# A fused cross-attention and mixture-of-experts layer: the unused experts' bias added per tile on VectorE, and the context means formed through joined weights with sums on GpSimd

## The reference, cut to what matters

```python
x = x + tanh(g_xattn) * xattn(layernorm(x), ctx, ctx, mask, ...)      # B=8, S=256, D=128, 16 heads of 64
x = x + tanh(g_ffn)   * ffn(layernorm(x), W1, b1, W2, b2, Wr, br)     # 8 experts, hidden 512

# xattn: the context has 1601 rows; mask and a causal triangle leave 256 of them to look at
scores = where(mask, -1e30, q @ k.T / 8); scores = where(causal, -1e30, scores)
out = (softmax(scores) @ v) @ Wo + bo

# ffn: each token has one expert, but every expert adds its bias path for every token
indices = argmax(softmax(x @ Wr + br))
for i in range(8):
    m = (indices == i)
    h = relu((x * m) @ W1[i] + b1[i])
    out = out + (h @ W2[i] + b2[i])
```

## Time and profile before

| | before |
|---|---|
| device time, median of 3 runs | 433.3 us (424.26, 433.30, 433.83) |
| profiled execution | 424.33 us, its span 422.7 us |
| mean granted TensorE clock | 0.972 of full |
| busy: PE / DVE / ACT / POOL | 384.2 / 283.7 / 241.5 / 193.5 us |
| busy share: PE / DVE / ACT / POOL | 91% / 67% / 57% / 46% |
| DMA moved | 25.23 MB |

### The profile page before, as it was taken

One profiled execution on the slowest core, in us unless ns is written; L12 is line 12 of the kernel. 1 busy time (PEld: TensorE's weight loads), 2 busy tenths in 40 slices (PEclk: granted clock), 3 DMA queues, 4 the chain that ended last, 5 costly groups with the idle time before them and its releaser, 6 DMA issues.

```text
span 422.7 us, 11118 instructions
## 1 busy us (share of the span) xinstructions
PE 384.2 (91%) x2881; PEld 301.9 (71%) x2881; DVE 283.7 (67%) x1283; ACT 241.5 (57%) x888; POOL 193.5 (46%) x353
## 2 busy tenths in 40 slices
PE   3959658899999999999999999999999969899992
PEld 2836446777787787778777778877776758788882
DVE  3289999469839866983987597498847855344440
ACT  2665533547748774874778387477735424455441
POOL 7069962145345553543655355354525322534332
PEclk9998998999999999999999999999999995899998
DMA  7892469000000000000000000000000046322210
GB/s 198 213 334 78 135 207 305 0 3 2 1 26 0 0 12 12 0 0 25 0 0 10 15 0 0 25 0 0 0 26 2 2 149 265 100 58 64 75 36 6
DMA packets 20553, 25.23 MB, mean 60 GB/s; under 512 B 3545, under 2 KB 16677, under 8 KB 20528
## 3 DMA queue, kind: packets, MB, share of 16 engines
q1 hardware_dynamic: 18544, 19.40, 15.4%
q0 software_dynamic: 1984, 5.53, 3.5%
HBM read 18.48 MB, written 6.90 MB: 60 GB/s over the span
## 4 chain that ended last, share of the span: by engine, by line
PE 57%; DVE 23%; issue 11%; DMA 2%; ACT 2%; DVEq 1%; another core or an unknown queue 1%; POOL 1%; SPq 1%; ACTq 0%; POOLq 0%
PE ps_kv L1110 11%; PE ps_o L1110 10%; PE ps_w L1110 10%; PE ps_s L1110 8%; PE ps_t L1110 7%; PE ps_t L1183 6%; DVE masked L706 5%; PE ps_q L1110 4%; DVE prob_T L725 3%; DVE neg_max L706 2%; DVE rs_t L659 1%; DVE row_fix L713 1%; DMA wv_s<-in_L_xattn_Wv 1%; DVE rows L765 1%; DVE rs_t L657 1%
## 5 line engine op out<-in xcount | busy, mean ns | idle before, releaser
L543 ACT ACTIVATE prob<-masked,neg_max 128x128 f32<-128x128 f32 (+1 forms) x256 | 113.4, 444 | 80.5 <-DVE neg_max L706 80.4
L416 POOL TENSOR_TENSOR prob<-prob,row_inv 128x128 f32<-128x128 f32 x128 | 51.0, 398 | 150.2 <-DVE row_inv L719 150.2
L706 DVE CUSTOM_DVE_ANT_0 masked<-ps_s,mask_now 128x128 f32<-128x128 f32 (+1 forms) x256 | 78.3, 353 | 20.5 <-PE ps_s L1110 16.6
L418 POOL TENSOR_TENSOR prob<-prob,row_inv 128x256 f32<-128x256 f32 x128 | 78.3, 611 | 0.0
L725 DVE COPY prob_T<-ps_t 128x384 f32<-128x384 f32 x128 | 67.6, 547 | 0.0
L1110 PE MATMUL ps_s<-k_T,q_T 64*128 64x128 f32 (+1 forms) x512 | 60.7, 356 | 6.5 <-DVE neg_max L706 6.4
L1183 PE MATMUL ps_t<-ident,prob 128*128 128x128 f32 x384 | 58.1, 286 | 4.8 <-POOL prob L418 2.8
L1183 PEld LDWEIGHTS ps_t<-ident,prob 128*128 128x128 f32 x384 | 41.6, 143 | 27.5 <-issue 17.8
L1110 PE MATMUL ps_o<-prob_T,v_nat 128*64 128x256 f32 (+1 forms) x512 | 56.4, 342 | 0.0
L543 ACT ACTIVATION_READ_ACCUMULATOR prob<-masked,neg_max 128x1 f32 x256 | 47.8, 187 | 0.0
L1110 PEld LDWEIGHTS ps_s<-k_T,q_T 64*128 64x128 f32 x512 | 34.5, 190 | 17.1 <-issue 15.8
(11 more groups left out here) (194 smaller groups left out, 602.9 us busy)
## 6 DMA issues: line engine op xcount, KB each, us to landing
ctx_ring<-in_ctx SPq DMA_DIRECT2D x8, 768.0 KB
ctx_ring<-sorted_rows SPq DMA_DIRECT2D x24, 128.5 KB, 2.1
sorted_rows<-pad_rows POOLq DMA_DIRECT2D x6, 385.5 KB, 3.9
packs<-in_L_ffn_W SPq DMA_DIRECT2D x1, 2048.0 KB
packs<-in_L_ffn_W SPq DMA_DIRECT2D x8, 256.0 KB
ctx_nat<-in_ctx SPq DMA_DIRECT2D x8, 128.0 KB, 4.0
x_nat<-in_x SPq DMA_DIRECT2D x1, 896.0 KB, 9.3
sorted_rows<-pad_rows SPq DMA_DIRECT2D x2, 385.5 KB
```

The costliest lines, as they stand in the source:

```text
L416: g.tensor_tensor(prob[:, slot, 0:P], prob[:, slot, 0:P], row_inv[:, slot, 0:1].to_broadcast([P, P]), ALU.mult).then_inc(prob_ready, 1)
L418: g.tensor_tensor(prob[:, slot, P:W3], prob[:, slot, P:W3], row_inv[:, slot, 1:2].to_broadcast([P, S]), ALU.mult).then_inc(prob_ready, 1)
L543: s.activation(prob[:, slot, lo:hi], masked[:, slot % 2, lo:hi], ACT.Exp, bias=neg_max[:, slot, t:t + 1], scale=-1.0, accum_out=row_sum[:, ...
L706: v.tensor_tensor_reduce(out=masked[:, slot % 2, lo:hi], in0=ps_s[slot % 2][:, lo:hi], in1=mask_now[:, lo:hi], scale=-SCALE, scalar=FLOOR, ...
```

## The change

**First part.** The per-tile selector product is gone. `rest` is computed earlier: the 32 small products all run inside batch 7 (`EMPTY_AT`), the small product in step 6, and in step 7 eight products (`rest_everywhere`) spread `rest` over all 128 partitions, in two PSUM banks that ScalarE copies to `rest_all`. VectorE adds the chosen expert's row of `rest_all`, times tanh(g_ffn), to each loaded tile (`rest_to`), and `finish` waits for that.

**Second part.** The eight contexts share one buffer, loaded one at a time: context 0 where it was, the others in a loop on SP after the experts' weights, each after the sum of the one before. GpSimd does both additions for every context, one context per batch (step 3, for the next batch; context 0 after step 0 of batch 0), VectorE one reduction per batch (step 6). In batch 0 PE transposes Wv (8 transposes in steps 2 and 3) and multiplies it by Wo once (step 4), and transposes `blind` to columns. Then each batch has one product for its mean and one through the joined weights, with two copies on ScalarE, and GpSimd adds blind x mean to the residual rows: `residual_of` has three operations instead of one and moves from step 1 to step 4 (step 7 in batch 0). The two `blind` products of each output projection are gone. The tiles no longer share memory with the context ring.

```diff
-            for b in range(B):
-                r = b % CTXR
-                wait(sp, ctx_sum_ready, b - CTXR + 1)
-                sp.dma_start(ctx_ring[:, r, 0:FULL], ctx_in[b, 0:FULL * P, :].rearrange("(p j) d -> p j d", p=P)
-                             ).then_inc(ld_ring[r], 16)
-                sp.dma_start(tail_ring[0:TAIL, r], ctx_in[b, FULL * P:SK, :]).then_inc(ld_ring[r], 16)
+            sp.dma_start(ctx_buf[:, 0:FULL], ctx_in[0, 0:FULL * P, :].rearrange("(p j) d -> p j d", p=P)
+                         ).then_inc(ld_ctx, 16)
+            sp.dma_start(ctx_buf[0:TAIL, FULL], ctx_in[0, FULL * P:SK, :]).then_inc(ld_ctx, 16)
             sp.dma_start(w1_s, w1.rearrange("e d f -> d e f")).then_inc(ld_ffn, 16)
             for e in range(E):
                 sp.dma_start(w2_s[:, e], w2[e].rearrange("(c p) d -> p c d", p=P)).then_inc(ld_ffn, 16)
             sp.dma_start(b2_s[:, :], b2).then_inc(ld_ffn, 16)
+            with sp.Fori(1, B) as b:
+                sp.wait_ge(ctx_sum_ready, b)
+                sp.dma_start(ctx_buf[:, 0:FULL], ctx_in[bass.ds(b, 1), 0:FULL * P, :].rearrange(
+                    "o (p j) d -> p (o j) d", p=P)).then_inc(ld_ctx, 16)
+                sp.dma_start(ctx_buf[0:TAIL, FULL:FULL + 1], ctx_in[bass.ds(b, 1), FULL * P:SK, :].rearrange(
+                    "o p d -> p o d")).then_inc(ld_ctx, 16)
 
 
...
 
-                r = b % CTXR
-                pool.wait_ge(ld_ring[r], 32 * (b // CTXR + 1))
-                n.up(g.tensor_tensor(ctx_ring[:, r, 0:6, :], ctx_ring[:, r, 0:6, :], ctx_ring[:, r, 6:12, :], ALU.add))
-                n.wait()
-                g.tensor_tensor(ctx_ring[:, r, 9:12, :], ctx_ring[:, r, 0:3, :], ctx_ring[:, r, 3:6, :], ALU.add
+                pool.wait_ge(ld_ctx, 32 * b + 32)
+                g.tensor_tensor(ctx_buf[:, 0:6, :], ctx_buf[:, 0:6, :], ctx_buf[:, 6:12, :], ALU.add
+                                ).then_inc(half_summed, 1)
+                pool.wait_ge(half_summed, b + 1)
+                g.tensor_tensor(ctx_buf[:, 9:12, :], ctx_buf[:, 0:3, :], ctx_buf[:, 3:6, :], ALU.add
                                 ).then_inc(csum_ready, 1)
 
             def residual_of(b):
 
                 wait(pool, x2_ready, 2 * b)
                 pool.wait_ge(ld_x[1], 16)
+                pool.wait_ge(y_kept, b + 1)
                 g.tensor_tensor(residual[:, :, :], x_nat[:, bass.ds(b * QT, QT), :],
-                                tg_bo[:, None, :].to_broadcast([P, QT, D]), ALU.add).then_inc(residual_ready, 1)
+                                tg_bo[:, None, :].to_broadcast([P, QT, D]), ALU.add).then_inc(base_ready, 1)
+                g.tensor_tensor(blind_y[:, :, :], tg_mean[:, None, :].to_broadcast([P, QT, D]),
+                                blind_col[:, bass.ds(b, 1), :].rearrange("p o t -> p (o t)")[:, :, None].to_broadcast(
+                                    [P, QT, D]), ALU.mult).then_inc(blindy_ready, 1)
+                pool.wait_ge(base_ready, b + 1)
+                pool.wait_ge(blindy_ready, b + 1)
+                g.tensor_tensor(residual[:, :, :], residual[:, :, :], blind_y[:, :, :], ALU.add
+                                ).then_inc(residual_ready, 1)
 
             def scatter(b):
 
...
                         if first:
                             pool.wait_ge(tgbo_ready, 1)
+                            pool.wait_ge(blind_kept, 1)
                         residual_of(b)
+                    if j == 3 and not last:
+                        sum_context(b + 1)
                     if j == 7 and not first:
                         scatter(b - 1)
-                    if first and j + 1 < len(POOL_SUMS):
-                        sum_context(POOL_SUMS[j + 1])
-            sum_context(0)
+                    if first and j == 0:
+                        sum_context(0)
...
+            def keep_mean(b):
+                act.wait_ge(mean_done, b + 1)
+                s.activation(ctx_mean[:, :], ps_mean, ACT.Copy).then_inc(mean_kept, 1)
+            def keep_y(b):
+                act.wait_ge(y_done, b + 1)
+                wait(act, residual_ready, b)
+                s.activation(tg_mean[:, :], ps_y, ACT.Identity, scale=tg[:, 0:1]).then_inc(y_kept, 1)
             def keep_x2T(b):
                 act.wait_ge(x2T_done, b + 1)
...
-                    if b in POOL_SUMS:
-                        dve.wait_ge(csum_ready, POOL_SUMS.index(b) + 1)
-                    n.wait()
-                    v.reduce_sum(ctx_sum[:, b, :], ctx_ring[:, r, 9:13, :].rearrange("p j d -> p d j"), AX.X
-                                 ).then_inc(ctx_sum_ready, 1)
+            def sum_context(b):
+                dve.wait_ge(csum_ready, b + 1)
+                wait(dve, mean_done, b)
+                v.reduce_sum(ctx_sum[:, :], ctx_buf[:, 9:13, :].rearrange("p j d -> p d j"), AX.X
+                             ).then_inc(ctx_sum_ready, 1)
 
             def bias_columns(step):
...
+                if here == 36 and not last:
+                    sum_context(b + 1)
                 if 4 <= here < 20:
                     second_norm(b - 1, here - 4)
...
+            def rest_to(tile, r, turn):
+                dve.wait_ge(tile_loaded[r], 16 * turn + 16)
+                v.scalar_tensor_tensor(out=tile_in[:, r, 0:D], in0=rest_all[:, bass.ds(expert, 1), :],
+                                       scalar=tg[:, 1:2], in1=tile_in[:, r, 0:D], op0=ALU.mult, op1=ALU.add
+                                       ).then_inc(based, 1)
             def finish(tile, r):
                 dve.wait_ge(y2_done, tile + 1)
+                dve.wait_ge(based, tile + 1)
                 v.scalar_tensor_tensor(out=tile_out[:, r, :], in0=ps_out[r % 2][:, 0:D], scalar=tg[:, 1:2],
                                        in1=tile_in[:, r, 0:D], op0=ALU.mult, op1=ALU.add).then_inc(out_ready, 1)
...
-            v.tensor_tensor(empty[:, :], empty[:, :], b2_s[:, :], ALU.add).then_inc(empty_kept, 1)
             expert = expert_of(0)
             weights_of(0, 0, 1)
 
-            dve.wait_ge(rest_done, 1)
-            v.tensor_tensor(rest[:, :], ps_rest, b2_s[:, :], ALU.add).then_inc(rest_ready, 1)
             expert = expert_of(1)
             weights_of(1, 1, 1)
             for step in range(6):
                 choose(B - 1, step)
+            dve.wait_ge(rest_kept, 2)
...
-            def output_projection(b, first):
+            def output_projection(b):
                 wait(pe, slots_ready, b)
-                if first:
-                    pe.wait_ge(y_kept, 2)
+                pe.wait_ge(y_kept, b + 1)
                 for t in range(QT):
                     for c in range(PAIRS):
                         if t == 0 and c >= PAIRS - 2:
                             pe.wait_ge(oT_kept, 8 * b + c + 1)
-                        mm(ps_w[:, t * P:(t + 1) * P], o_T[:, c, t * P:(t + 1) * P], wo_s[:, c, :],
-                           start=c == 0, stop=False)
-                    if first:
-                        pe.wait_ge(y_kept, 3)
-                    last = mm(ps_w[:, t * P:(t + 1) * P], blind[:, t * P:(t + 1) * P],
-                              mean_rows[:, bass.ds(b, 1), :], start=False, stop=True)
+                        last = mm(ps_w[:, t * P:(t + 1) * P], o_T[:, c, t * P:(t + 1) * P], wo_s[:, c, :],
+                                  start=c == 0, stop=c == PAIRS - 1)
                 last.then_inc(wo_done, 1)
...
+            def wv_transposes(half):
+                wait(pe, wvT_kept, half)
+                for i in range(PAIRS // 2):
+                    c = half * (PAIRS // 2) + i
+                    last = t_.transpose(ps_w[:, i * P:(i + 1) * P], wv_s[:, c * P:(c + 1) * P], ident[:, :])
+                last.then_inc(wvT_done, 1)
...
+            def wv_through_wo():
+                pe.wait_ge(wvT_kept, 2)
+                pe.wait_ge(ld_wo, 16)
+                pe.wait_ge(blind_ready, 1)
+                for c in range(PAIRS):
+                    mm(ps_wvo, wv_T[:, c, :], wo_s[:, c, :], start=c == 0, stop=c == PAIRS - 1)
+                for t in range(QT):
+                    last = t_.transpose(ps_blind[:, t * B:(t + 1) * B], blind[:, t * P:(t + 1) * P], ident[0:B, 0:B])
+                last.then_inc(wvo_done, 1)
             def mean_of(b):
 
                 pe.wait_ge(ctx_sum_ready, b + 1)
-                mm(ps_mean[:, b:b + 1], ctx_sum[:, b, :], mean_w[:, :]).then_inc(mean_done, 1)
-            def means_through_wv(lo, hi):
-                pe.wait_ge(mean_kept, 1)
-                for c in range(lo, hi):
-                    last = mm(ps_u[:, c * B:(c + 1) * B], wv_s[:, c * P:(c + 1) * P], ctx_mean[:, :])
-                last.then_inc(u_done, 1)
-            def means_through_wo():
-                pe.wait_ge(u_kept, 1)
-                for c in range(PAIRS):
-                    last = mm(ps_y, u_T[:, c, :], wo_s[:, c, :], start=c == 0, stop=c == PAIRS - 1)
-                last.then_inc(y_done, 1)
+                wait(pe, x2_ready, 2 * b)
```

(49 more changed lines are left out.)

160 lines of the change are left out of this document (84 added, 76 removed).

## The result

The changed kernel takes 407.08 us (median of 4 executions, 405.27 to 410.71) beside 430.52 us for the kernel before (median of 4, 424.26 to 433.83). Two of those four, 433.30 and 433.83 us, are of the slower kind that some executions show, so the ratio leaves them out and compares the means 407.5 and 426.0 us: 0.957, 95% interval 0.943 to 0.971. A second measurement gives 404.81 beside 422.18 us: 0.957, interval 0.954 to 0.961. The prediction's 401 us lies 6 us under the first median; both lie in its range of 389 to 413.

What follows compares the result with a forecast made beforehand. PE was taken to bound loop batches and tiles, VectorE batch 0. 424.3 - 2.3 - 14.2 - 3.0 + 3.5 - 9.7 = 398.6 us; raised to 401 for unexplained run differences, range 389 to 413.

Steps and rivals of the forecast that it cites:

- the 9 us that it could not explain: Whole kernel: median of three earlier runs, 433.3 us, lay 9.0 above the profiled execution; the forecast was raised to 401.
- last sign: Whole kernel: prediction fails if loop batches grow by more than they lose, or VectorE or a load ends the tile-loop waits.
- third step: Batches 1 to 6: 0.5 us gained each, 3.0 in all; wrong if PE waits over 0.5 for `prob` or `rows`.
- Start-up, 2.3 gained: Before batch 0's first transposes: context 0's sum moves behind step 0's scaling, gaining 2.3 us, bounds 0 and 3.4.
- Batch 0, 14.2 gained: Batch 0: less VectorE work shortens it from 56.7 to 42.5 us, gaining 14.2, bounds 9 and 16.6.
- the floors: Batch 0: estimated minimum work, 40.1 us for PE and 36.9 for VectorE, plus the output projection, about 43.
- covered, but with nothing to spare: Batch 0: context 1's load and sum let pair 6 be scaled by 52 us, about when PE wants it.
- this case: Batch 0: rival that context 1 comes late, losing 5 us of the gain, giving 404 us; chance 0.09.
- the rival that had 0.10: Loop batches: GpSimd becomes moderately late, each loses 1.1 us instead of gaining 0.5, giving 408 us; chance 0.10.
- Batch 7, 3.5 lost: Batch 7: sixteen small products moved onto PE's path ahead of the slots cost 3.6; net 3.5 us lost, bounds 1.5 and 5.
- Tiles, 9.7 gained: Tiles: removing the selector product saves 0.41 us in each of 23 tiles; 9.7 us gained net, bounds 5.8 and 11.
- The rule of equal time for few rows: Tiles: few rows take a full product's time, so the selector costs 0.25, not 0.41; gain 3.7 us less.

Runs made afterwards that it cites:

- experiment 1: Changed kernel with GpSimd's addition of the next context moved from step 3 to 4, residual operations from step 4 to 6, in batches 1 to 7: 397.69 us, ratio 0.944.
- experiment 5: Changed kernel with 24 of the 32 products for the empty columns left out of batch 7: 403.83 us, ratio 0.953.
- experiment 8: Changed kernel with context sums moved later, half the empty-column products and the spreading before tile 0, VectorE's additions for them ahead of its last norm: 389.32 us, ratio 0.921.
- experiment 10: Separate kernel computing nothing of the layer: TensorE products of differing row counts, VectorE forms beside GpSimd; alternating 128 and 8 rows took 0.42 us a product, 128 alone 0.22.

## Why the prediction was right on the whole, and where not

**The sum.** It foresaw 25.7 us of gain. Against the 426.0 us above the first measurement shows 18.5, the second shows 17.4 (422.18 to 404.81); the two profiles' spans show 13.6 and 20.9 (the first is of the slowest of its four executions). For an execution like the profiled one it said 398.6 us, and the two profiled ones took 410.71 and 403.60. The forecast of 401 adds 2.4 us for the 9 us that it could not explain, which brought it nearer by luck: the changed kernel's four executions lie within 5.5 us. The sum came as near as it did because its misses had both signs: 5.1 and 3.0 us too much gain in batch 0 and 6.7 and 6.6 in the loop batches, against 2.5 and 5.4 too little in the tiles. By its own last sign ("fails if the loop batches grow by more than they lose") its third step failed (TensorE waits 1.29 us for `rows` there, where over 0.5 was to mean wrong).

**1. Start-up, 2.3 gained: about right in size.** TensorE's wait of 2.34 us for scaled probabilities is gone from its first transposes in both profiles. The first profile still gains nothing (30.09 for 29.22): its TensorE was 1.8 us later than the kernel before's already at the scores ahead of them (26.30 for 24.47) and then at the lower clock until 29.6. The second begins at 27.47, and the nine later kernels that keep this part at 25.0 to 26.9, for "about 27" predicted. With one profile of the kernel before I can't say how much of this is the execution.

**2. Batch 0, 14.2 gained: right number, wrong about the cover.** Kernels with context 1's sum in step 5 take 42.37 us, 14.3 less than before: the 42.5 was right as a number, though neither engine fills it: VectorE is busy for 34.34 us of it and TensorE for 38.89, where the floors had 36.9 and 40.1. The step that failed is "covered, but with nothing to spare". Its two figures were short: the reduction stands at a fixed place of VectorE's batch and ran at 47.3 (45.4 in the second profile), not 43; and the load took 6.1 us from issue to GpSimd's start (5.0 in the second profile), where I had taken 3.9 from a DMA window, which ends with the transfer; GpSimd starts about 1 us behind the last packet (53.58 to 54.64). The queue behind the wait was named rightly; the clock's fall after it, in the first profile, wasn't counted. I gave this case 0.09, with the sum of its own figures at zero slack; it should have been the likeliest.

**3. Loop batches, 0.5 gained each: wrong sign, 0.6 lost.** All of the difference is the hold of `rows`, which the prediction named, bounded at 1.1 and charged at 0.2 by the mean excess of another instruction. It is the mechanism of the rival that had 0.10, at a lower price: 0.6 lost a batch, not 1.1. The mean was the mis-sized term: a hold is not an average, it is decided by what starts first, and here the order of the two queues makes it the same in each batch: 1.13 us a batch (experiment 1). Without it the batches gain 0.53, where the sum had 0.7 ahead of that charge.

**4. Batch 7, 3.5 lost: right**, 3.1 and 3.5. Leaving out 24 of the 32 products takes 3.5 to 3.9 us off (experiment 5), so they do cost most of their time ahead of the slots, and the wait before tile 0 was 2.06 and 4.3 us where about 4 was forecast. With half of them and the spreading behind the last projection batch 7 takes 33.89 us (experiment 8), 0.9 more than before the change.

**5. Tiles, 9.7 gained: right cause, size too small.** 12.2 us in the first profile, 15.1 in the second. The mis-sized term is the selector: 0.61 us a tile, not its own row's 0.41. The row shows what one instruction takes; what two changes of rows cost lies in its neighbours too. VectorE had room, as forecast, in the loop: TensorE is busy for all of 20.12 us there. In the written-out tiles it had less: TensorE waits 1.11 us there (0.91 and 1.10 in the second profile) for VectorE's copy of the weights, a wait that the kernel before doesn't have.
The rule of equal time for few rows (the Trainium skill, TensorE: Matmul & The Clock Gate, Why this matters for your kernels) holds in a run of such products (experiment 10), and by it the part would have come out too small. The rule that bears on the tile is another page's: a change of tiling mode drains the engine (the Trainium skill, TensorEngine Tiling (Array Packing), Key Properties). The runs fit it, if going from 128 to 8 rows is such a change, and put 0.19 us on it at the full clock.
